# Graph attention layer 1 by four column groups while its gather is still running, the node's own part on ScalarE, and the carry between partitions applied to one fetched row per partition

## The chip, the cores and the metric

The program runs on one core of one Trainium2 chip. The metric is the device time of one execution in microseconds. The kernel before was timed in three runs: median 4706.49 us, lowest 4698.56, highest 4711.57. One further execution was recorded by the hardware profiler; all rows below are from it.

## The reference, cut to what matters

A graph of 100,000 nodes and 25,000 edges sorted by destination passes through four layers (gated, two-head attention twice, cosine attention, message passing), each followed by a layer norm. The change is in the first of the two attention layers:

```python
logits = jax.nn.leaky_relu(alpha_s[src] + alpha_d[dst], 0.2)
m = jax.ops.segment_max(logits, dst, num_segments=N)
e = jnp.exp(logits - m[dst])
s = jax.ops.segment_sum(e, dst, num_segments=N)
a = e / s[dst]
out = jax.ops.segment_sum(h[src] * a[:, :, None], dst, num_segments=N)
```

Every node also has an edge to itself (the "own" part). Only nodes that are a destination of some edge need this work; the others are finished in an earlier, dense pass.

## The kernel before

**Layout.** The 25,000 sorted edges lie as 125 partitions x 200 columns (P, J), 200 consecutive edges per partition. A segment (all edges of one destination) is a run along the columns, and may go on into the next partition. Sums over segments are scans along the columns (`tensor_tensor_scan`) followed by a carry between the partitions: the last column is transposed on TensorE, scanned, and transposed back (`carry_dve`, L829 to L839). `cont`, `last` and `more` mark where runs go on and end, `reach_f` which columns a carry reaches.

**Blocks.** The program is a row of blocks; every engine ends its part of a block before the next block starts. In order: constants and start, degrees (L1030), dense node pass (L1093), gate layer (L1225), attention layer 1 (L1379, the block that is changed), attention layer 2 (L1493), cosine layer (L1591), message layer (L1696).

**The block of attention layer 1.** GpSimd (POOL) gathers one row of 69 floats per edge from the table `x1_rows` into `xa` (a view of `edge_rows`): 8 indirect DMAs for the last 4 partitions (the "tail"), then 200 of 121 rows, one per column (L215), all counted by one semaphore. VectorE (DVE) meanwhile runs the first part of a bitonic sort that a later layer needs (L938 to L989), then `attention_dve` (L1307): it spreads the destination's term (L1312 to L871), waits for the whole gather (L1319), makes segment maxima, exponentials and segment sums over all 200 columns and both heads, and inverts the sums. The gathered rows are weighed by the exponentials, the first 80 columns on GpSimd and the other 120 on VectorE (`weigh1`, L1365, L1366). Then 128 scans, one per head and feature, sum them along the columns (L881), with one carry per head.

After that comes a loop over 25 chunks of 8 columns (NC), two to a loop iteration, with two sets of buffers. For each chunk VectorE does ten operations on 125x512 (own part, carry, sum and division for each head) into `e_dup`; TensorE transposes the eight 125x128 tiles (L1427), ScalarE (ACT) copies them from PSUM (L1450), TensorE multiplies them by `heads_w`, with a bias matmul ahead of every bank (L463, L1437), and ScalarE copies the result out in six pieces (L1458, L1459), whence SyncE (SP) stores it into `h_rows` by two DMAs of 462 KB and 54 KB. The product uses one set of three PSUM banks, so the next product waits for these six copies. SyncE also loads the node's own rows `r_x` for every chunk. Layer 2 gathers from `h_rows`, so its block starts when all is stored.

## Time and profile before

| | |
|---|---|
| median of 3 runs | 4706.49 us (4698.56 to 4711.57) |
| the profiled execution, its own time | 4719.72 us |
| its span, first to last instruction | 4717.9 us |
| busy: TensorE, VectorE, ScalarE, GpSimd | 1437.9, 2476.2, 959.6, 2857.0 us |
| mean granted TensorE clock | 0.529 of full |

Times in rows are microseconds from the start of the span. 1.8 us lie outside the span. A row of a timeline gives start, duration, engine, line, operation, what it writes <- reads, count, and in brackets how long the engine was idle before and who released it. A granted clock of 0.50 is TensorE at 1.2 GHz, 1.00 is 2.4 GHz.

### The profile page before, as it was taken

What the parts mean: (1) busy time and instruction counts of PE and PEld (TensorE: products, weight loads), DVE (VectorE), ACT (ScalarE), POOL (GpSimd) and SP (SyncE); (2) the same over time, 40 slices, a digit from 0 to 9 for tenths busy, and PEclk for the clock granted to TensorE, in tenths of its full rate; (3) what the DMA queues carried; (4) which work ended last, traced back from release to release, by engine and by line L of the source; (5) the groups of instructions that cost most, each with busy time, mean ns of one, the idle gap of its engine ahead of it and who ended that gap; (6) DMA issues with size and microseconds to landing.
All of it is one profiled execution on the core that took longest, in us unless ns stands there. A gap on an engine that the chain in (4) does not pass through costs nothing. (4 is left out here: it accounts for less than half of the span.)

```text
span 4717.9 us, 35071 instructions
## 1 busy us (share of the span) xinstructions
PE 1437.9 (30%) x5413; PEld 1244.8 (26%) x5413; DVE 2476.2 (52%) x5048; ACT 959.6 (20%) x2420; POOL 2857.0 (61%) x2507
## 2 busy tenths in 40 slices
PE   2888067772041002753400000000000067154121
PEld 2888057772030001542300000000000045143121
DVE  4565056661587848762078843334864434352453
ACT  1555034441020000210100011221000034123110
POOL 7777777777205760017750057777248877787687
PEclk8555555555555555555555555555555556556555
DMA  3666145542011100224403345554001145344011
GB/s 81 191 188 186 34 116 139 139 135 48 5 44 39 27 16 20 85 72 104 123 7 90 99 115 141 151 147 127 5 10 19 19 122 161 100 111 112 16 17 17
DMA packets 260931, 398.20 MB, mean 84 GB/s; under 512 B 98227, under 2 KB 104370, under 8 KB 260842
## 3 DMA queue, kind: packets, MB, share of 16 engines
q1 hardware_dynamic: 171022, 322.96, 22.6%
q0 software_dynamic: 89856, 74.77, 9.1%
q14 instruction: 47, 0.39, 0.0%
q8 instruction: 6, 0.10, 0.0%
HBM read 185.60 MB, written 212.64 MB: 84 GB/s over the span
## 5 line engine op out<-in xcount | busy, mean ns | idle before, releaser
L806 PE MATMUL banks<-ident,cross_in 125*2 125x125 f32 (+3 forms) x26 | 10.5, 405 | 2015.3 <-DVE cross_in L829 1366.4
L593 PE MATMUL banks<-node_w,x_t 65*125 65x200 f32 x1600 | 551.5, 536 | 0.0
L806 PEld LDWEIGHTS banks<-ident,cross_in 125*2 125x2 f32 (+3 forms) x26 | 3.0, 117 | 2019.9 <-DVE cross_in L829 1369.5
L593 PEld LDWEIGHTS banks<-node_w,x_t 65*125 65x125 f32 x1600 | 515.1, 330 | 3.9
L215 POOL DMA_INDIRECT edge_rows<-x_rows,src_i x400 | 414.7, 1037 | 127.8 <-issue 127.8
L273 POOL DMA_INDIRECT x_rows<-r_x,src_scat_i x200 | 258.3, 1291 | 120.4 <-issue 60.6
L273 POOL DMA_INDIRECT norm_rows<-edge_rows,scat_i x200 | 259.1, 1295 | 74.2 <-issue 74.2
L273 POOL DMA_INDIRECT out_dram<-n_out,scat_i x200 | 250.3, 1251 | 78.9 <-issue 60.7
L215 POOL DMA_INDIRECT edge_rows<-x_rows,dst_place_i x200 | 231.6, 1158 | 64.5 <-issue 64.5
L215 POOL DMA_INDIRECT edge_rows<-in_x_dram,src_i x200 | 221.8, 1109 | 69.1 <-issue 65.4
L636 DVE TENSOR_REDUCE n_var<-n_sq 125x8 f32<-125x512 f32 x125 | 85.6, 686 | 324.0 <-ACT n_sq L650 323.9
L215 POOL DMA_INDIRECT edge_rows<-in_x_dram,dst_i x200 | 214.7, 1074 | 63.7 <-issue 63.7
L215 POOL DMA_INDIRECT edge_rows<-x_rows,norm_s x200 | 213.1, 1066 | 64.5 <-issue 64.5
L215 POOL DMA_INDIRECT edge_rows<-x_rows,key_i x200 | 213.7, 1068 | 61.0 <-issue 61.0
L215 POOL DMA_INDIRECT tops<-norm_rows,src_i x200 | 207.7, 1038 | 63.7 <-issue 63.7
L215 POOL DMA_INDIRECT edge_rows<-h_rows,src_i x200 | 204.9, 1025 | 63.8 <-issue 63.8
L1146 ACT ACTIVATE n_sq<-n_c 125x512 f32<-125x512 f32 x100 | 62.9, 629 | 828.6 <-DVE n_c L1131 828.6
L236 POOL DMA_INDIRECT x_t<-h_rows,src_tail_i x8 | 8.0, 1006 | 337.0 <-POOLq L1379 334.9
L236 POOL DMA_INDIRECT x_t<-x_rows,gray_i x16 | 16.8, 1052 | 301.5 <-DMA gray_i<-sorted_pairs 296.9
L881 DVE TENSOR_TENSOR_SCAN edge_rows<-cont,edge_rows 125x200 f32<-125x200 f32 x384 | 186.2, 570 | 11.1 <-POOL edge_rows L1373 10.9
L455 PE MATMUL banks<-ident,own 125*65 125x125 f32 x400 | 96.5, 422 | 313.3 <-DVE own L529 313.3
L742 DVE TENSOR_REDUCE n_var<-n_sq 125x8 f32<-125x512 f32 x100 | 68.5, 685 | 220.7 <-ACT n_sq L727 220.7
(346 smaller groups left out, 5045.9 us busy)
## 6 DMA issues: line engine op xcount, KB each, us to landing
h_rows<-r_h SPq DMA_DIRECT2D x125, 462.0 KB
x_rows<-r_x SPq DMA_DIRECT2D x125, 241.5 KB
x_rows<-r_x SPq DMA_DIRECT2D x125, 224.0 KB
r_x<-x_rows SPq DMA_DIRECT2D x125, 224.0 KB
x_rows<-n_out SPq DMA_DIRECT2D x125, 224.0 KB
n_in<-in_x_dram SPq DMA_DIRECT2D x100, 224.0 KB
n_c<-x_rows SPq DMA_DIRECT2D x100, 224.0 KB
out_dram<-n_out SPq DMA_DIRECT2D x100, 224.0 KB
```

Source lines behind the costliest of these rows:

```text
L215: g.indirect_dma_start(out=to[0:MAIN, j, :], out_offset=None, in_=table, in_offset=bass.IndirectOffsetOnAxis(ap=idx[0:MAIN, j:j + 1], axis ...
L236: g.indirect_dma_start(out=self.rows[:, j, :], out_offset=None, in_=self.table, in_offset=bass.IndirectOffsetOnAxis(ap=self.idx[:, j:j + 1 ...
L273: g.indirect_dma_start(out=table, out_offset=bass.IndirectOffsetOnAxis(ap=idx[:, j:j + 1], axis=0), in_=frm[:, j, :] if len(frm.shape) == ...
L455: done = pe.transpose(bank[4 + 2 * u + c // 4][0:D + 1, c % 4 * P:c % 4 * P + P], rows[:, c, :], ident[0:P, 0:P])
L593: done = pe.matmul(product[h][:, n // 2, n % 2, :], x_t[u][:, at:at + P], node_w[:, :], start=True, stop=True)
L636: dve.tensor_reduce(n_var[u][:, :], n_sq[u][:, :, :], AX, ALU.add).then_inc(sx3.var, 1)
L742: dve.tensor_reduce(n_var[u][:, :], n_sq[u][:, :, :], AX, ALU.add).then_inc(so.var, 1)
L806: pe.transpose(bank[0][0:cols, 0:rows], frm, ident[0:rows, 0:rows]).then_inc(s_tout, 1)
L881: done = dve.tensor_tensor_scan(rows[:, :, f], cont[:, :], rows[:, :, f], 0.0, ALU.mult, ALU.add)
L1146: nc.scalar.activation(flat(n_sq[u][:, :, :]), flat(n_c[u][:, :, :]) if frm is None else frm(u), ACT.Square, scale=D ** -0.5).then_inc(s.s ...
```

## The change

1. The block works by four **column groups** of 80, 64, 32 and 24 columns (10, 8, 4 and 3 chunks). The gather counts each group on its own semaphore, and VectorE starts a group when its columns are there. The order of the 200 gathers stays.
2. In each group a **running softmax**: peaks are scanned first, every column's sum is rescaled to the new peak by the scan itself (its multiplier is `scales` instead of `cont`), and a group's scans start from the last column of the group before (a per-partition scalar as initial value). So there are 4 x 128 feature scans of 80, 64, 32 and 24 columns instead of 128 of 200. The spreading of maxima and sums back over the segment is gone. All weighing is on VectorE.
3. `merge_own` makes two factors per column and head: `mixes` for the sum and for the own part.
4. In the chunk, **ScalarE makes the own part**: 16 activations of 125x64, each with a per-partition scale read from `mixes`, into `e_dup`. VectorE does two products (ahead) and two additions. The order on TensorE and ScalarE is written out by hand, chunk by chunk.
5. No carry is added to the chunks. `e_dup` of every chunk is also stored (table ED, 512 KB a chunk). At the end the carry between the partitions is worked out (`ends_in`), **one row per partition** (the first segment end in it, the only one that a carry can change) is fetched from ED by an indirect DMA, mended, multiplied by `heads_w` and scattered over its row in `h_rows`.
6. Elsewhere: `own_logits` (the spreading of the destination's term) goes ahead of the sort; comparisons read the integer keys and save three casts in three blocks; the degree block finds the first segment ends (`first_ends`, nine small operations); the cosine layer uses the same four groups instead of five. 

The core of the diff (blank lines left out, `...` for what is left out; `ends_in` computes maxima and masses of the first segment ends, one carry for the peaks and, for each head, three transposes of 65 rows with one scan):

```diff
-GROUPS = (0, 10, 18, 22, 24, 25)
+GROUPS = (0, 10, 18, 22, 25)
...
+        def running_softmax(dve, s, rows, at, n, sums, weigh):
+            a, b = (NC * c for c in groups[n])
+            c = slice(a, b)
+            for h in range(H):
+                done = dve.tensor_tensor(scales[:, 2 + h, c], rows[:, c, at + h], dens[h][:, c], ALU.add)
+            v.link(done)
+            for h in range(H):
+                done = dve.scalar_tensor_tensor(scales[:, 2 + h, c], scales[:, 2 + h, c], 0.2, scales[:, 2 + h, c], ALU.mult, ALU.max)
+            v.link(done)
+            for h in range(H):
+                done = dve.tensor_tensor_scan(peaks[:, h, a + 1:b + 1], pen_f[:, c], scales[:, 2 + h, c], peaks[:, h, a:a + 1], ALU.add, ALU.max)
+            v.link(done)
+            for h in range(H):
+                dve.tensor_tensor(scales[:, 2 + h, c], scales[:, 2 + h, c], peaks[:, h, a + 1:b + 1], ALU.subtract)
+                done = dve.tensor_tensor(scales[:, h, c], peaks[:, h, a:b], peaks[:, h, a + 1:b + 1], ALU.subtract)
+            v.link(done)
+            for h in range(H):
+                done = dve.scalar_tensor_tensor(scales[:, h, c], scales[:, h, c], 0.0, pen_f[:, c], ALU.min, ALU.add)
+            done.then_inc(s.args, 1)
+            dve.wait_ge(s.exps, 2 * n + 1)
+            for h in range(H):
+                done = dve.tensor_tensor_scan(masses[:, h, c], scales[:, h, c], scales[:, 2 + h, c], masses[:, h, a - 1:a] if a else 0.0, ALU.mult, ALU.add)
+            v.link(weigh(dve, c))
+            for h in range(H):
+                for f in range(D):
+                    done = dve.tensor_tensor_scan(sums[h][:, c, f], scales[:, h, c], sums[h][:, c, f], sums[h][:, a - 1, f:f + 1] if a else 0.0, ALU.mult, ALU.add)
+            v.link(done)
+        def merge_own(dve, s, n, share):
...
+            for k in range(2 * H):
+                done = dve.scalar_tensor_tensor(mixes[:, k, w], mixes[:, k, w], share, scales[:, 2 + k % H, c], ALU.mult, ALU.mult)
+            done.then_inc(s.args, 1)
+            dve.wait_ge(s.args, 3 * n + 3)
...
+        def ends_in(dve, s, sums):
...
-                gather_all(g, tail_xa, s1.gathered, src_place_i)
-                g.wait_ge(s1.gathered, ALL)
-                g.wait_ge(s1.exps, 1)
-                weigh1(g, pool, GPSIMD_COLS).then_inc(s_shared, 1)
+                tail_xa.fetch(g)
+                for n, (start, end) in enumerate(groups):
+                    cols = range(start * NC, end * NC)
+                    gather(g, xa, X1, src_place_i, s_got[n], cols[0:TAIL_STEPS[0]])
+                    if n == 0:
+                        tail_xa.put_down(g)
+                    gather(g, xa, X1, src_place_i, s_got[n], cols[TAIL_STEPS[0]:])
+                    if n == 0:
+                        tail_xa.place(g, s_first)
+                for u in range(U):
+                    g.wait_ge(s1.mixed[u], ROWS_DONE * ((ECH + 1 - u) // 2))
+                g.wait_ge(s1.turned, ECH)
+                g.indirect_dma_start(out=first_mixed.rearrange("p h f -> p (h f)"), out_offset=None, in_=ED,
+                                     in_offset=bass.IndirectOffsetOnAxis(ap=first_i[:, :], axis=0)).then_inc(s_first, 16)
+                for u in range(U):
+                    g.wait_ge(s1.stored[u], ROWS_DONE * ((ECH + 1 - u) // 2))
+                g.wait_ge(s1.row, ECH + 1)
+                g.indirect_dma_start(out=H2, out_offset=bass.IndirectOffsetOnAxis(ap=first_scat_i[:, :], axis=0), in_=first_row, in_offset=None,
+                                     bounds_check=last_row(g, ROWS), oob_is_err=False).then_inc(s_first, 16)
...
                 sort_fill_dve(dve)
+                own_logits(dve)
                 sort_start_dve(dve)
                 sort_dve(dve, PARTS[0], held[0], held[1])
...
+                dve.wait_ge(s_first, 16)
+                for n, (start, end) in enumerate(groups):
+                    dve.wait_ge(s_got[n], got_done(n, 1))
+                    running_softmax(dve, s1, xa, D + 1, n, sums, weigh)
+                    merge_own(dve, s1, n, 1.0)
+                    for i in range(start, end):
+                        u, c, w = i % 2, slice(i * NC, i * NC + NC), slice((i - start) * NC, (i - start) * NC + NC)
+                        parts = (n_sq[u], n_in[u])
+                        for h in range(H):
+                            done = dve.tensor_tensor(parts[h][:, :, :], sums[h][:, c, :], wide(mixes[:, h, w]), ALU.mult)
+                        v.link(done)
+                        dve.wait_ge(s1.own, i + 1)
+                        for h in range(H):
+                            done = dve.tensor_tensor(e_dup[u][:, :, h, :], e_dup[u][:, :, h, :], parts[h][:, :, :], ALU.add)
+                        done.then_inc(s1.x, 1)
+                ends_in(dve, s1, sums)
...
-                    sum_rows_dve(dve, sums[h], carry_rows[h])
-
-                def body(i, us):
-                    for u in us:
-                        dve.wait_ge(s1.loaded[u], ROWS_DONE * i + ROWS_DONE)
-                        if not is_first(i):
-                            dve.wait_ge(s1.turned, 2 * i - 1 + u)
-                        for h in range(H):
-                            tmp = (n_sq, n_in)[h][u][:, :, :]
-                            v.link(dve.tensor_tensor(tmp, r_x1[u][:, :, 0:D], wide(chunk(selfs[h], i, u)), ALU.mult))
-                            add_carry(dve, n_out[u][:, :, :], sums[h], carry_rows[h], i, u, n_c[u][:, :, :])
-                            v.link(dve.tensor_tensor(tmp, tmp, n_out[u][:, :, :], ALU.add))
-                            done = dve.tensor_tensor(e_dup[u][:, :, h, :], tmp, wide(chunk(dens[h], i, u)), ALU.mult)
-                        done.then_inc(s1.x, 1)
-                pairs(nc.vector, ECH, body, v)
+                    dve.tensor_scalar(n_sq[0][:, h, :], first_mixed[:, h, :], first_keep[:, h:h + 1], None, ALU.mult)
...
+                for start, end in groups:
+                    for i in range(start, end):
+                        turn_chunk(i)
+                        if i > start:
+                            heads_chunk(i - 1)
+                    heads_chunk(end - 1)
+                ends_pe(pe)
...
+                def own_chunk(i, start):
+                    u = i % 2
+                    act.wait_ge(s1.loaded[u], ROWS_DONE * (i // 2 + 1))
+                    if i >= 2:
+                        act.wait_ge(s1.turned, i - 1)
+                        act.wait_ge(s1.mixed[u], ROWS_DONE * (i // 2))
+                    for c in range(NC):
+                        w = (i - start) * NC + c
+                        for h in range(H):
+                            done = nc.scalar.activation(e_dup[u][:, c, h, :], r_x1[u][:, c, 0:D], ACT.Copy, scale=mixes[:, 2 + h, w:w + 1])
...
+                for n, (start, end) in enumerate(groups):
+                    logits_act(act, s1, n)
+                    if n:
+                        turned_chunk(start - 1)
+                        row_chunk(start - 1)
+                    merged_act(act, s1, n)
+                    act.wait_ge(s1.args, 3 * n + 3)
+                    for i in range(start, end):
+                        own_chunk(i, start)
+                        if i > start:
+                            turned_chunk(i - 1)
+                            row_chunk(i - 1)
+                turned_chunk(ECH - 1)
+                row_chunk(ECH - 1)
+                ends_act(act, s1)
...
+                for i in range(ECH):
+                    u = i % 2
+                    sp.wait_ge(s1.x, i + 1)
+                    rows_dma(sp, edge_rows(ED, i // 2, u, 2 * D), flat(e_dup[u][:, :, :, :].rearrange("p c h f -> p c (h f)")), s1.mixed[u])
+                    if i + U < ECH:
+                        load(i + U)
+                    sp.wait_ge(s1.row, i + 1)
+                    rows_dma(sp, edge_rows(H2[0:EDGES], i // 2, u, W2ROW), flat(r_h2[u][:, :, :]), s1.stored[u])
```

On ScalarE, in the block of layer 1. Before, the loop's first chunks, 2 copies of each transposed pair for two chunks, then the six copies of a product (`own`, `r_h`):

```order
L1450 COPY n_t<-banks 128x500 [waits s_att1_turned]
L1450 COPY n_t<-banks 128x500
L1450 COPY o_t<-banks 128x500 [waits s_att1_turned]
L1450 COPY o_t<-banks 128x500
L1458 COPY own<-banks 125x12 [waits s_att1_h2]
L1459 COPY r_h<-banks 125x396
L1458 COPY own<-banks 125x12
L1459 COPY r_h<-banks 125x396
L1458 COPY own<-banks 125x8
L1459 COPY r_h<-banks 125x264
```

Now, from the third chunk of a group (`mixed`: its earlier `e_dup` is stored; `loaded`: own rows are there):

```order
L1654 ACTIVATE e_dup<-r_x,x_t 125x64 [waits s_att1_mixed0,s_att1_turned,s_att1_loaded0]
L1654 ACTIVATE e_dup<-r_x,x_t 125x64 x15
L1660 COPY o_t<-banks 128x500 [waits s_att1_turned]
L1660 COPY o_t<-banks 128x500
L1670 COPY own<-banks 125x12 [waits s_att1_h2]
L1671 COPY r_h<-banks 125x396
L1670 COPY own<-banks 125x12
L1671 COPY r_h<-banks 125x396
L1670 COPY own<-banks 125x8
L1671 COPY r_h<-banks 125x264
```

The sixteen activations of chunk i stand ahead of the copies of chunk i-1, and behind those of chunk i-2's product. At a group's start 32 activations (two chunks) stand together.

On TensorE, at the same place; `turned_sb`, `row` and `x` are the semaphores of ScalarE's two sets of copies and of VectorE's `e_dup`. Before, inside the loop (two transposes, two products):

```order
L1427 MATMUL banks<-ident,e_dup 128x125 [waits s_att1_turned_sb,s_att1_x]
L1427 MATMUL banks<-ident,e_dup 128x125 x7
L463 MATMUL banks<-h_bias,ones 125x396 [waits s_att1_row,s_att1_turned_sb]
L1437 MATMUL banks<-heads_w,n_t 125x132 x3
L463 MATMUL banks<-h_bias,ones 125x396
L1437 MATMUL banks<-heads_w,n_t 125x132 x3
L463 MATMUL banks<-h_bias,ones 125x264
L1437 MATMUL banks<-heads_w,n_t 125x132 x2
L463 MATMUL banks<-h_bias,ones 125x396 [waits s_att1_row,s_att1_turned_sb]
L1437 MATMUL banks<-heads_w,o_t 125x132 x3
```

Now:

```order
L1612 MATMUL banks<-ident,e_dup 128x125 [waits s_att1_turned_sb,s_att1_x]
L1612 MATMUL banks<-ident,e_dup 128x125 x7
L464 MATMUL banks<-h_bias,ones 125x396 [waits s_att1_row,s_att1_turned_sb]
L1624 MATMUL banks<-heads_w,o_t 125x132 x3
L464 MATMUL banks<-h_bias,ones 125x396
L1624 MATMUL banks<-heads_w,o_t 125x132 x3
L464 MATMUL banks<-h_bias,ones 125x264
L1624 MATMUL banks<-heads_w,o_t 125x132 x2
```

The transposes of chunk i now stand ahead of the product of chunk i-1, one to one; before, two transposes stood ahead of two products.

## Rows read from the trace of the kernel before

**Rows 1.** VectorE's timeline, block of layer 1 (from 1440 us)

```profile
1455.41 0.29 DVE L946 CAST o_t<-att 128x256 f32<-128x256 int32 x1 [11.74 <-DMA att<-edge_places]
...
1655.25 0.33 DVE L1312 COPY dens_selfs<-own 125x200 f32<-125x200 f32 x1
...
1726.14 0.51 DVE L1319 TENSOR_TENSOR head<-edge_rows,dens_selfs 125x200 f32<-125x200 f32 x1 [63.86 <-DMA edge_rows<-x_rows,src_i]
...
1740.94 9.08 DVE L1334 COPY dens_selfs<-head 125x200 f32<-125x200 f32 x2 [1.21 <-ACT dens_selfs L1345]
...
1766.92 8.16 DVE L1365 TENSOR_TENSOR edge_rows<-edge_rows,head 125x7680 f32<-125x7680 f32 x1
...
1783.31 29.92 DVE L881 TENSOR_TENSOR_SCAN edge_rows<-cont,edge_rows 125x200 f32<-125x200 f32 x64
...
1848.96 0.69 DVE L1407 TENSOR_TENSOR n_sq<-r_x,dens_selfs 125x512 f32<-125x512 f32 x1
```

**Rows 2.** GpSimd's timeline, same block: last gather, first weighing

```profile
1723.43 1.02 POOL L215 DMA_INDIRECT edge_rows<-x_rows,src_i  x1 [0.30 <-issue]
1741.07 8.84 POOL L1365 TENSOR_TENSOR edge_rows<-edge_rows,head 125x5120 f32<-125x5120 f32 x1 [16.62 <-ACT dens_selfs L1345]
```

**Rows 3.** TensorE's timeline in the chunk loop

```profile
1863.13 1.93 PE L1427 MATMUL banks<-ident,e_dup 125*128 125x125 f32 x8 [5.09 <-DVE e_dup L1410]
...
1872.45 0.55 PE L463 MATMUL banks<-h_bias,ones 3*125 3x396 bf16 x1 [1.56 <-ACT r_h L1459]
...
1878.12 2.13 PE L1427 MATMUL banks<-ident,e_dup 125*128 125x125 f32 x16
1880.75 0.38 PE L463 MATMUL banks<-h_bias,ones 3*125 3x396 bf16 x1 [0.51 <-ACT n_t L1450]
```

**Rows 4.** ScalarE's timeline in the chunk loop

```profile
1870.92 0.17 ACT L1458 COPY own<-banks 125x12 f32<-125x12 f32 x1 [4.78 <-PE banks L1437]
...
1884.28 0.17 ACT L1458 COPY own<-banks 125x12 f32 x1 [2.62 <-PE banks L1437]
```

**Rows 5.** Stretches: us; busy (count) of PE, PEld, DVE, ACT, POOL; clock; DMA share; GB/s

```profile
1864.00:1868.00 4.00, 4.00 (x15) 2.76 (x14) 3.67 (x6) 1.05 (x2) 0.00 (x0) 0.50 0.26 69
...
1880.00:1884.00 4.00, 3.49 (x22) 2.40 (x20) 0.00 (x0) 1.66 (x4) 0.00 (x0) 1.00 0.69 198
...
2240.00:2260.00 20.00, 12.47 (x44) 8.89 (x44) 0.00 (x0) 3.88 (x7) 15.43 (x16) 0.50 0.42 115
```

**Rows 6.** VectorE's groups by shape, 1438 to 2095 us: busy, mean ns | idle

```profile
L881 DVE TENSOR_TENSOR_SCAN edge_rows<-cont,edge_rows 125x200 f32<-125x200 f32 x128 | 61.5, 559 | 0.1
...
L832 DVE TENSOR_TENSOR_SCAN crossed<-pass_r_t,banks 2x125 f32<-2x125 f32 x2 | 0.8, 402 | 0.1
L871 DVE SCALAR_TENSOR_TENSOR tops<-reach_r,carry_in,tops 125x200 f32<-125x200 f32 x2 | 0.8, 424 | 0.0
...
L1315 DVE SCALAR_TENSOR_TENSOR dens_selfs<-dens_selfs 125x200 f32<-125x200 f32 x2 | 0.7, 368 | 0.1
```

**Rows 7.** ScalarE's activations, gate layer: timeline (two with a pointer operand)

```profile
1288.90 0.49 ACT L1150 ACTIVATE n_sd<-n_var,eps 125x8 f32<-125x8 f32 x2
```

**Rows 8.** ScalarE's groups by shape, gate layer and layer 1

```profile
L1146 ACT ACTIVATE n_sq<-n_c 125x512 f32<-125x512 f32 x3 | 1.9, 629 | 56.9 <-DVE n_c L1131 56.9
L1150 ACT ACTIVATE n_sd<-n_var,eps 125x8 f32<-125x8 f32 x2 | 0.5, 292 | 0.0
L1345 ACT ACTIVATE head<-head 125x200 f32<-125x200 f32 x2 | 0.6, 362 | 296.1 <-DVE dens_selfs L1330 296.1
```

**Rows 9.** Timeline at the end of the block, VectorE's last `e_dup`, GpSimd's next gather

```profile
2078.22 0.69 DVE L1410 TENSOR_TENSOR e_dup<-n_in,dens_selfs 125x512 f32<-125x512 f32 x1
2093.74 1.04 POOL L236 DMA_INDIRECT x_t<-h_rows,src_tail_i  x1 [334.87 <-POOLq L1379]
```

**Rows 10.** Timeline at the end of the degree block

```profile
69.37 0.26 DVE L1028 CAST scat_i<-head 125x200 int32<-125x200 f32 x1
77.64 1.05 POOL L215 DMA_INDIRECT edge_rows<-in_x_dram,src_i  x1 [3.73 <-POOLq L1030]
```

More of the change, by code:

```diff
@@ L920, in build @@
         held = [t[:, :, :].rearrange("p k f -> p (k f)") for t in (att1, att2)]
-        def turns_before(step):
-            return sum(what == "turn" for what, _ in STEPS[:step])
         def sort_sp(sp):
@@ L953, in sort_dve @@
         def sort_dve(dve, part, to_k, to_d):
-            now, turns = 0, turns_before(part[0])
+            now = 0
             for n in range(*part):
@@ new lines, in logits_act, with merged_act, first_at @@
+        def logits_act(act, s, n):
+            a, b = (NC * c for c in groups[n])
+            act.wait_ge(s.args, 3 * n + 1)
+            nc.scalar.activation(scales[:, :, a:b], scales[:, :, a:b], ACT.Exp).then_inc(s.exps, 1)
+        def merged_act(act, s, n):
+            w = NC * (groups[n][1] - groups[n][0])
+            act.wait_ge(s.args, 3 * n + 2)
+            nc.scalar.activation(mixes[:, :, 0:w], mixes[:, :, 0:w], ACT.Exp).then_inc(s.exps, 1)
+        def first_at(dve, plane_of, to):
+            for h in range(H):
+                v.link(dve.tensor_tensor(heads[h][:, :], plane_of(h), first_end[:, :], ALU.mult))
+                done = dve.tensor_reduce(to[:, h:h + 1], heads[h][:, :], AX, ALU.add)
+            v.link(done)
@@ new lines, in ends_act, with ends_pe @@
+        def ends_act(act, s):
+            act.wait_ge(s.args, 3 * len(groups) + 1)
+            nc.scalar.activation(end_exp, end_exp, ACT.Exp)
+            nc.scalar.activation(first_exp, first_exp, ACT.Exp).then_inc(s.exps, 1)
+        def ends_pe(pe):
+            carry_pe(pe, H, "max")
+            for _ in range(H):
+                transpose_pe(pe, cross_in[0:P, 0:D + 1], P, D + 1)
+                transpose_pe(pe, cross_in[0:P, 0:D + 1], P, D + 1)
+                transpose_pe(pe, crossed[0:D + 1, 0:P], D + 1, P)
@@ L1379, in build @@
+        crossings["bank"] = bank[7]
+        first_mixed, first_row = e_dup[1][:, 0, :, :], r_h2[1][:, 0, :]
         with nc.Block() as block:
@@ new lines, in _ @@
+                done.then_inc(s1.x, 1)
+                v.link(dve.tensor_scalar(heads[0][:, :], first_end[:, :], 1.0, -1.0, ALU.subtract, ALU.mult))
+                dve.wait_ge(s1.row, ECH + 1)
+                for k in range(4):
+                    v.link(dve.tensor_tensor(own4[:, :, k], own4[:, :, k], heads[0][:, :], ALU.mult))
+                for k in range(4):
+                    v.link(dve.scalar_tensor_tensor(own4[:, :, k], first_end[:, :], first_row[:, 2 * D + k:2 * D + k + 1], own4[:, :, k], ALU.mult, ALU.add))
@@ new lines, in heads_chunk @@
+                def heads_chunk(i):
+                    u = i % 2
+                    pe.wait_ge(s1.turned_sb, i + 1)
+                    if i:
+                        pe.wait_ge(s1.row, i)
+                    for c in range(NC):
+                        if c % 3 == 0:
+                            cols = min(3, NC - c) * W2ROW
+                            add_bias(pe, bank[4 + c // 3][0:P, 0:cols], h2_bias[:, 0:cols])
+                        done = pe.matmul(h2_slot(c), turned_pair[u][c // 4][:, c % 4 * P:c % 4 * P + P], heads_w[:, :],
+                                         start=False, stop=c % 3 == 2 or c == NC - 1)
+                    done.then_inc(s1.h2, 1)
@@ new lines, in turned_chunk, with row_chunk @@
+                def turned_chunk(i):
+                    act.wait_ge(s1.turned, i + 1)
+                    for b in range(2):
+                        done = nc.scalar.copy(turned_pair[i % 2][b], bank[2 * (i % 2) + b][:, 0:NC // 2 * P])
+                    done.then_inc(s1.turned_sb, 1)
+                def row_chunk(i):
+                    u = i % 2
+                    act.wait_ge(s1.h2, i + 1)
+                    if i >= 2:
+                        act.wait_ge(s1.stored[u], ROWS_DONE * (i // 2))
+                    for b, cols in enumerate((3, 3, 2)):
+                        at = bank[4 + b][0:P, 0:cols * W2ROW]
+                        nc.scalar.copy(own4[:, i * NC + 3 * b:i * NC + 3 * b + cols, :], at.rearrange("p (c w) -> p c w", w=W2ROW)[:, :, 2 * D:W2ROW])
+                        done = nc.scalar.copy(flat(r_h2[u][:, 3 * b:3 * b + cols, :]), at)
+                    done.then_inc(s1.row, 1)
```

246 lines of the change are left out of this document (148 added, 98 removed).

## The prediction

> **What bounds the kernel now.** I read the timelines of the block that is changed first, since the chain of waits over the whole run only names its last part, and asked which engine each stretch waits for. VectorE sorts until 1655.25 us, needs 7 us to spread the destination's term, and then sits idle for 63.86 us until the gather has landed at 1726.1 [rows 1]; the last of the 200 gathers is issued at 1723.4 [rows 2]. From there VectorE alone sets the pace: softmax, weighing and 128 scans until 1848.96 [rows 1], then 25 chunks until 2078.9, which is 9.2 us a chunk. 14.8 us after the last `e_dup` the next block's first gather starts (2093.74) [rows 9]. Everything after that block is unchanged, so what the change is worth is by how much it moves 2093.74. The reader is to see two prizes: the idle 64 us, and a chunk that costs VectorE ten operations. One more lies hidden: two copies took 9.08 us while GpSimd was weighing [rows 1, 2].
>
> **The change, part by part.** I rebuild the block's time from 1655.2 on, when the sort ends.
>
> *What goes ahead of the sort.* `own_logits` takes about 7 us (1655.25 to 1662.28, where the idle time began). It moves into an idle time of 11.74 us, in which VectorE waits for the keys [rows 1]. So the sort ends as before. Were that cover gone, it would cost 7 us.
>
> *Group phases on VectorE.* Group 1's 80 columns are fetched long before 1655: at 1.32 us a gather, 1655 is some 52 gathers ahead of the last [rows 2], so about 148 columns are there; group 2 needs 144, and groups 3 and 4 come later than 1723 anyway. No group waits for the gather.
> - Scans. 200 columns cost 29.92/64 = 0.467 us from start to start [rows 1], 559 ns each as a single duration; 125 columns took 402 ns [rows 6]. The slope is 157/75 = 2.09 ns a column, which leaves 0.05 us fixed. From the second group on, the initial value is a per-partition scalar: such an operand made a three-operand operation 424 instead of 368 ns [rows 6], so +0.056. 128 scans: 27.8 us at 80 columns, 30.7 at 64, 22.1 at 32, 20.0 at 24: together 100.6. Before: 60 and two carries. Bounds: without the scalar's cost 79; 20% more for short instructions 120.
> - Weighing. 7680 elements took 8.16 us [rows 1]: 10.9, 8.7, 4.4, 3.3 for two heads: 27.3. Before, VectorE paid 16.3 and the collision above.
> - Small operations: about 25 a group, at 368 ns for 200 columns [rows 6] and so some 0.24 us for 80 and 0.18 for 24, with two trips to ScalarE of half a microsecond and two reciprocals: an estimate of 8.4, 7.4, 5.3 and 4.8 us.
>
> That is 46.9, 46.7, 31.7 and 28.0 us.
>
> *A wait that the order on ScalarE adds.* Its exponentials for the next group stand behind the product copies of the last chunk but one. These come 9.1 us after VectorE's last `e_dup` (next paragraph), and VectorE needs only 2.3, 1.6, 1.5 us to get there. So it idles 6.8, 7.5 and 7.6 us at the three later groups.
>
> *The chunk.* VectorE's ten operations become four, two of them ahead. But each engine now stands behind the next one round. TensorE transposes chunk i before the product of i-1, so that product waits for `e_dup` of i; ScalarE makes the own part of i+1 only after it has copied the product of i-1. One turn round:
> - ScalarE, 16 activations with a scale from a pointer. Two with a pointer took 0.49 us, 292 ns each, so 0.198 from start to start at 8 elements [rows 7, 8]; 362 ns at 200 and 629 at 512 elements give 0.86 ns an element [rows 8], so 0.246 at 64. I take 0.24: 3.9 us with the last one's end. Lower bound, from the exponential without its pointer cost: 0.17, 2.8 us.
> - VectorE's two additions of 125x512: 0.61 + 0.69 = 1.3.
> - TensorE, eight transposes and the product: from 1863.13 to ScalarE's first copy at 1870.92, 7.8 us at half clock [rows 3, 4].
> - ScalarE's six copies: 1870.92 to TensorE's next start at 1872.45, less one handover: 1.3 [rows 3, 4].
> - Three handovers: 0.1.
>
> Sum: 14.4 us, against 9.2 before. The first two chunks of a group come faster, since their 32 activations stand together: 5.3 us to the first `e_dup`, 3.9 more to the second. So 8 + 6 + 2 + 1 = 17 full rounds are paid.
>
> *SyncE.* A round stores 512 KB of ED and 528 KB of `h_rows` and loads 276 KB, 1.3 MB. At 198 GB/s [rows 5] that is 6.6 us. What was issued in one round is needed a round later; it lies hidden under 14.4, and would decide at a round of about 9.
>
> *The end.* After the last `e_dup` two products are still to come: 7.8 + 1.3, the copies of the last pair 1.0, the product 5.9: 16.0. Only then is TensorE free for the carries of `ends_in`: eight crossings and some forty small operations, 11.5 us by the crossings and operations above. Fetching the row of ED from 10 us on is hidden by that. The mended row through TensorE and ScalarE: 3. The scatter, one gather's 1.0 us [rows 2] and its landing, beside eight operations on `own4`: 4. Closing the block: 3. Together 37.7, where it was 14.8. Bounds: 30 and 46.
>
> **The sum.** 1655.2; first group 46.9 + 5.3 + 3.9 + 8 x 14.4 = 171.3; second 6.8 + 46.7 + 9.2 + 86.4 = 149.1; third 7.5 + 31.7 + 9.2 + 28.8 = 77.2; fourth 7.6 + 28.0 + 9.2 + 14.4 = 59.2. The last `e_dup` ends at 2112.0, the next block's gather starts at 2149.7 instead of 2093.7: 56 us later. Elsewhere: `first_ends` adds about 2 us to VectorE in the degree block, which ends at 69.6 there, while GpSimd's gathers go on until 73.9 and hold the block [rows 10]; with that cover gone it would cost 2. The three saved casts and one group less in the cosine layer give under 1 us each. The profiled execution took 4719.7, so 4775.7; it lay 13 us above the median, and I forecast against the median: 4706.5 + 56 = **4762**.
>
> **A rule that speaks against it.** In the chunk loop TensorE was busy for 7.8 us on end after 5.09 idle [rows 3], and was granted 0.50 in it [rows 5]; only after the next product, with 1.56 us between, did it get full speed (1.00). In the projections, at 62% busy in short bursts, it stayed at 0.50 [rows 5]. A round has 7.8 busy and 6.6 idle, so I count at half clock. The Trainium skill ("TensorE: Matmul & The Clock Gate", Part 1) says that half rate is the default and sustained work releases it; by that, some rounds would be at 2.4 GHz, which is the first rival.
>
> **Rivals.**
> - *TensorE at full clock in the rounds.* For it: the grants above. Eight transposes then take 1.07 (half of 2.13) and the product 3.53 (1880.75 to 1884.28) [rows 3, 4], 3.2 us less a round; 17 rounds 54, the three idle times 10, the end 6: 70 in all, which is 14 us more than the 56 that the change costs: 4692, on the edge of faster. It decides when four fifths of the rounds are fast (56 of 70). Against it: the burst after 5.09 us of idleness was slow from end to end.
> - *Cheap operands.* If neither the scalar of the scans nor the pointer of the activations costs anything: 21 + 1.1 x 25 = 49 us less, 4713. The rows with such operands speak against it.
> - *The round is longer than its parts*, because ED's stores delay the loads or the activations run at their full 0.33: 2 us more a round, 4800.
> - *The change doesn't do what it says.* The gather is then still waited for. It can't be: 148 columns are there at 1655.
>
> **Chances.** Forecast 0.66, full clock 0.14, cheap operands 0.08, longer round 0.12. 0.3% of this time is 14 us, about what a measurement can tell from no change. Slower by more: forecast and longer round, 0.78. Cheap operands come out at 4713, the same; the full clock lies on the edge and is split, with a little for both together: 0.12 same, 0.10 faster. The range of the likeliest alone, from the bounds of scans, activations and the end, is 4725 to 4800; to 8 in 10 it reaches to the edge of the full clock and of the longer round: 4695 to 4812.
>
> **What would show it.** Right: VectorE starts on the logits of group 1 at about 1655 with no idle time for the gather; full rounds of 14.4 us with VectorE idle for over 10 of them and released by ScalarE; clock 0.50 there; about 7 us idle before the exponentials of groups 2 to 4; the next block at about 2150. Wrong: clocks near 1.00 in the rounds, activations 0.17 apart, scans of 24 columns well off 0.16, or VectorE waiting for `mixed` or `loaded`.

## The result, and the profile after

The changed kernel takes 4757.69 us (median of 3 runs, 4755.54 to 4764.99) against 4706.49: ratio 1.0114, 95% interval 1.0086 to 1.0143, so slower by 51 us. Forecast were 4762 and slower. A repeat gave 1.0097 (1.0069 to 1.0125). On three other chips the kernel before and all versions took 6280 to 6490 us; on the one of them where the changed kernel was timed, the change cost 146 us (below).

The next block's first gather is issued at 2152.18 us, 58.4 later than before [rows 9]; 56.0 were forecast. The two profiled spans differ by 38.0 only, because the profiled execution of before held one gather issue for 19.32 us, late in the program. Timeline of before, GpSimd:

```profile
4146.12 1.18 POOL L215 DMA_INDIRECT edge_rows<-x_rows,dst_place_i  x1 [0.30 <-issue]
4147.30 0.61 POOL L241 DMA_DIRECT2D tail_md<-x_t  x1
4148.21 19.32 POOL L215 DMA_INDIRECT edge_rows<-x_rows,dst_place_i  x1 [0.30 <-issue]
```

That gather was issued 18.3 us later than the usual step would have it, and 38.0 + 18.3 = 56.3. So behind the block of layer 1 the changed kernel gains 2 us on net (58.4 to 56.3), and ahead of it 1.7 (the sort's end, below). The medians differ by 51 and not by 56; the three timed runs of before lie 13 us apart, so these 5 us can't be told from scatter.

The start of the groups, timeline of the changed kernel. VectorE goes from the sort's last copy into the logits with no idle time, where before it waited 63.86 us [rows 1]:

```profile
1653.35 0.29 DVE L987 COPY att<-o_t 128x256 f32<-128x256 f32 x1
1653.55 0.49 DVE L1420 TENSOR_TENSOR x_t<-edge_rows,dens_selfs 125x80 f32<-125x80 f32 x2
...
1832.16 0.59 DVE L1437 TENSOR_TENSOR_SCAN x_t<-x_t 125x64 f32<-125x64 f32 x2 [7.14 <-ACT x_t L1475]
...
1980.91 0.46 DVE L1437 TENSOR_TENSOR_SCAN x_t<-x_t 125x32 f32<-125x32 f32 x2 [7.55 <-ACT x_t L1475]
...
2060.23 0.43 DVE L1437 TENSOR_TENSOR_SCAN x_t<-x_t 125x24 f32<-125x24 f32 x2 [7.65 <-ACT x_t L1475]
```

The three bracketed times are the idle that ScalarE's order adds (forecast 6.8, 7.5, 7.6). VectorE's groups in the block, by shape (busy, mean ns | idle):

```profile
L1441 DVE TENSOR_TENSOR_SCAN edge_rows<-x_t,edge_rows 125x64 f32<-125x64 f32 x128 | 31.4, 340 | 0.0
L1441 DVE TENSOR_TENSOR_SCAN edge_rows<-x_t,edge_rows 125x80 f32<-125x80 f32 x128 | 28.4, 312 | 0.0
L1441 DVE TENSOR_TENSOR_SCAN edge_rows<-x_t,edge_rows 125x32 f32<-125x32 f32 x128 | 23.7, 274 | 0.0
L1441 DVE TENSOR_TENSOR_SCAN edge_rows<-x_t,edge_rows 125x24 f32<-125x24 f32 x128 | 21.9, 272 | 0.0
L1583 DVE TENSOR_TENSOR e_dup<-e_dup,n_sq 125x512 f32<-125x512 f32 x25 | 17.3, 693 | 214.0 <-ACT e_dup L1654 214.0
```

The last row is where the time went: VectorE stood 214 us idle in front of its additions, released each time by ScalarE's own part. One full round, timeline of all engines:

```profile
1736.58 0.69 DVE L1583 TENSOR_TENSOR e_dup<-e_dup,n_sq 125x512 f32<-125x512 f32 x1 [11.92 <-ACT e_dup L1654]
...
1737.93 1.93 PE L1612 MATMUL banks<-ident,e_dup 125*128 125x125 f32 x8 [6.66 <-DVE e_dup L1583]
...
1745.73 0.17 ACT L1670 COPY own<-banks 125x12 f32<-125x12 f32 x1 [8.32 <-PE banks L1624]
...
1746.95 3.95 ACT L1654 ACTIVATE e_dup<-r_x,x_t 125x64 f32<-125x64 f32 x16
...
1751.01 0.69 DVE L1583 TENSOR_TENSOR e_dup<-e_dup,n_sq 125x512 f32<-125x512 f32 x1 [11.92 <-ACT e_dup L1654]
```

Follow the starts: additions, TensorE 1.35 us later, ScalarE's row copies 7.80 after that, the 16 activations 1.22 later, the next additions 4.06 later: 14.43. Each bracket names the one before it, and the activations have none, since ScalarE goes into them straight from its row copies: it is a ring. TensorE's clock in the round before it (stretch; busy of PE, PEld, DVE, ACT, POOL; clock; DMA share; GB/s):

```profile
1723.00:1738.00 15.00, 7.83 (x28) 5.81 (x29) 3.08 (x6) 6.10 (x24) 11.64 (x12) 0.50 0.45 119
```

The end of the block, timeline of the changed kernel:

```profile
2111.84 0.68 DVE L1583 TENSOR_TENSOR e_dup<-e_dup,n_in 125x512 f32<-125x512 f32 x1
...
2127.44 1.21 POOL L1549 DMA_INDIRECT e_dup<-x_mixed_edge_rows,first_i  x1 [368.36 <-DMA x_mixed_edge_rows<-e_dup]
2128.47 0.41 PE L808 MATMUL banks<-ident,cross_in 125*2 125x125 f32 x1
2128.95 0.06 DVE L837 MEMSET crossed<- 2x1 f32 x1 [13.40 <-PE banks L808]
...
2143.61 1.23 POOL L1554 DMA_INDIRECT h_rows<-r_h,first_scat_i  x1 [14.96 <-issue]
2152.18 1.03 POOL L237 DMA_INDIRECT x_t<-h_rows,src_tail_i  x1 [7.34 <-POOLq L1533]
```

The last `e_dup` is done at 2112.5 (forecast 2112.0); the carries stand 13.40 us behind two products; 39.7 us to the next gather (forecast 37.7).

### The profile page after: what moved, and what is told of

Its sections match the earlier page's. It is cut to its first block and busy times, and to the rows that moved or that the text cites. A ratio compares the mean times of both kernels' runs of the same rounds, so it can differ in the third digit from the quotient of the medians.

```text
span 4755.9 us, 35197 instructions
## 1 busy us (share of the span) xinstructions
PE 1450.2 (30%) x5415; PEld 1250.0 (26%) x5415; DVE 2424.0 (51%) x5411; ACT 1056.3 (22%) x2828; POOL 2858.5 (60%) x2507
## 5 line engine op out<-in xcount | busy, mean ns | idle before, releaser
L808 PE MATMUL banks<-ident,cross_in 125*2 125x125 f32 (+4 forms) x26 | 10.9, 419 | 1829.1 <-DVE cross_in L831 1180.1
L216 POOL DMA_INDIRECT edge_rows<-x_rows,src_i x400 | 453.6, 1134 | 125.3 <-issue 125.3
L216 POOL DMA_INDIRECT edge_rows<-x_rows,dst_place_i x200 | 214.5, 1073 | 63.9 <-issue 63.9
L1163 PE MATMUL banks<-ident,n_in 125*128 125x125 f32 x200 | 54.1, 428 | 386.5 <-DVE n_in L1968 282.5
```

What stands on the lines that cost most here:

```text
L216: g.indirect_dma_start(out=to[0:MAIN, j, :], out_offset=None, in_=table, in_offset=bass.IndirectOffsetOnAxis(ap=idx[0:MAIN, j:j + 1], axis ...
L808: pe.transpose(crossings["bank"][0:cols, 0:rows], frm, ident[0:rows, 0:rows]).then_inc(s_tout, 1)
L1163: done = pe.transpose(to[:, c * P:(c + 1) * P], flat(frm[:, 2 * c:2 * c + 2, :]), ident[0:P, 0:P])
```

## The experiments

"Block" is from the first transposes of layer 1 to the next block's first gather: 445.2 us in the changed kernel, 441.8 in its repeat. A round is given from one chunk's transposes to the next one's. Eight of the twelve runs fell on chips where the kernel before took 6304 to 6346 us; there rounds and blocks are compared rather than totals. The block can be compared between the chips: the changed kernel's is 444.7 us on such a chip. A thirteenth kernel, without the stores of the mixed rows (`e_dup`), gave no result.

**Own part ahead (`e1_own_ahead`).** ScalarE's order:

```diff
-    for i in range(start, end):
+    for i in range(start, min(start + 2, end)):
         own_chunk(i, start)
-        if i > start:
-            turned_chunk(i - 1)
-            row_chunk(i - 1)
+    for i in range(start, end - 1):
+        turned_chunk(i)
+        if i + 2 < end:
+            own_chunk(i + 2, start)
+        row_chunk(i)
```

> ScalarE writes the own part of chunk i+2 before it copies out the rows of chunk i, so two chunks' own parts are ready at the start of a group; nothing is left out. Theory A (the round of 14.42 us is a ring of order: own part 3.9, two additions 1.3, transposes and product 7.8, row copies 1.3, each waiting for the one before): the own part leaves the ring, and what is left of it is product 5.9, row copies 1.3, transposed copies 1.05, about 8.4 us. But SyncE still issues the store of the mixed rows of chunk i behind the rows of chunk i-1, and the own part of i+2 waits for that store (issued 2.3 us after the row copies, landing near 5): round 10.3 to 10.8, so 17 rounds give 4757.7 - 17*3.9 = about 4692 (4685 to 4700). Rival B (the stores of the mixed rows do not bind, only ScalarE's order does): about 4657, the same as the next kernel. Rival C (the group phases and the tail are the cost, the rounds are covered): 4755 to 4760.

Measured: rounds of 11.6 to 12.2 us behind a first one of 13.4 to 14.0, block 392.6, 49 less than the repeat's. The time on this chip was 6380.17 against 6306.56, ratio 1.0108 (1.0066 to 1.0149). The ring is broken, but a second one binds: 10.3 to 10.8 us and 66 us less were expected, with the wait for the mixed store as its last link. That link was wrong. Timeline:

```profile
2476.48 3.93 ACT L1654 ACTIVATE e_dup<-r_x,x_t 125x64 f32<-125x64 f32 x16 [5.84 <-DMA r_x<-x_rows]
```

ScalarE waits for the load of the own rows (`r_x`), the last of the three transfers that SyncE issues after the row copies, not for the mixed store ahead of it; it does so for 5.4 to 6.1 us in every full round but the first.

**Store and load first (`e1b_own_ahead_store_first`).** As above, and on SyncE:

```diff
...
         load(i + U)
-    sp.wait_ge(s1.row, i + 1)
-    rows_dma(sp, edge_rows(H2[0:EDGES], i // 2, u, W2ROW), flat(r_h2[u][:, :, :]), s1.stored[u])
+    if i:
+        store(i - 1)
+store(ECH - 1)
```

> As the kernel before, and SyncE issues the mixed store and the next load of chunk i before the row store of chunk i-1; nothing is left out. Theory A: round 8.4 to 8.6 us, 17 * 5.9 = 100 us less: 4657 (4645 to 4670), which is below the kernel before the change (4706.5). Rival D (1.3 MB of loads and stores in a round are what binds then): a round of 10 or more, over 4680. Rival E (TensorE, now busy 7.8 of 8.5 us, is granted its full clock): a round of about 6.5, under 4635. Rival C: 4755 to 4760.

(`store(i)` is the two lines that are taken out.) Measured: rounds of 6.7 to 8.3, block 335.0: 107 less, where 100 were expected. Stretch of its first group:

```profile
2433.00:2507.00 74.00, 63.94 (x251) 48.72 (x251) 25.27 (x49) 52.73 (x207) 0.00 (x0) 0.68 0.53 164
```

TensorE is busy 86% and is now the bound; a part of its work got the full clock (mean 0.68), so that single rounds came down to 6.7; 8.4 to 8.6 were expected. DMA moves 164 GB/s instead of 119. ScalarE still waits for a load of own rows once in each group, 1.35 to 2.21 us at its third chunk, 7.2 us in all, and TensorE doesn't stand still for it. So the mixed store doesn't bind here; whether a kernel without it would be faster isn't shown. The same kernel was run once more on another chip (`e1c_store_first_again`); its block was 332.6.

> The store-first kernel unaltered, to have its time beside a kernel before of about 4707 us. From the traces: first transposes to the next block's first gather 335 us in it and 441.8 us in the repeat of the changed kernel, so 107 us less than that one's 4753.6: 4647 (4638 to 4656), ratio 0.987. Rival D (what the rounds give is lost in the rest of the program): over 4680.

On that chip the kernel before took 6304.48: 6317.53, ratio 1.0018 (0.9997 to 1.0038), and 6313.35 with 1.0005 (0.9981 to 1.0029) the first time. So the expected total of 4647 stays untested.

**Own part on VectorE (`e2_own_on_vector`).**

```diff
+    dve.wait_ge(s1.loaded[u], ROWS_DONE * (i // 2 + 1))
...
+    for h in range(H):
+        done = dve.tensor_tensor(e_dup[u][:, :, h, :], r_x1[u][:, :, 0:D], wide(mixes[:, 2 + h, w]), ALU.mult)
     v.link(done)
-    dve.wait_ge(s1.own, i + 1)
...
-        own_chunk(i, start)
```

> The own part is written by two products of 125x512 on VectorE (0.69 us each) in place of the 16 activations on ScalarE; orders of TensorE, ScalarE and SyncE stay, nothing is left out. Theory A: ScalarE's part leaves the ring and VectorE runs ahead of it; round 8.4 to 9.3, group starts 2 us shorter each: 4757.7 - 17*5.5 - 8 = about 4656 (4640 to 4675). Rival F (the ring is the one-to-one order of TensorE and the row copies, whoever writes the own part): 4757.7 - 17*1.3 = 4735 or more, for 3.9 us on ScalarE become 2.6 on VectorE in the same ring.

Measured: mostly rounds of 10.7 and 7.6 in turn, mean 8.9 over the 17; block 350.9, 91 less; ratio 1.0044 beside 1.0089 and 1.0108 of the two that keep a ring through ScalarE. The own part costs VectorE 1.29 us here and the round is 5.5 us shorter, so what it cost before was its place in ScalarE's order. What is left is VectorE's wait for the same late load (6.8 to 8.6 us in the longer rounds).

**Two activations (`e3_two_activations`).**

```diff
-    for c in range(NC):
-        w = (i - start) * NC + c
-        for h in range(H):
-            done = nc.scalar.activation(e_dup[u][:, c, h, :], r_x1[u][:, c, 0:D], ACT.Copy, scale=mixes[:, 2 + h, w:w + 1])
+    w = (i - start) * NC
+    for h in range(H):
+        done = nc.scalar.activation(e_dup[u][:, :, h, :], r_x1[u][:, :, 0:D], ACT.Copy, scale=mixes[:, 2 + h, w:w + 1])
```

> The own part of a chunk is written by 2 activations of 125x512 (0.63 us each) instead of 16 of 125x64, all 8 columns of a chunk scaled by the first column's weight, so the own part of seven of eight columns is wrongly weighted; order unchanged. Theory A: the ring loses 3.95 - 1.26 = 2.7 us: round 11.7, 17 rounds 46 us, group starts 3.9 us each, 16: 4696 (4688 to 4705). Rival C (ScalarE's time is not in the ring): 4755 to 4760. Rival G (the ring is set by waits for the store of mixed rows, not by ScalarE's work): above 4735.

This kernel leaves out the factors of seven of eight columns, so its results are wrong; the amount of data is the same. Measured: rounds of 11.86 (forecast 11.7) while the clock was 0.50, 10.1 to 10.2 in the second half of group 2, where it was 0.61 on the mean; block 385.3, 56 less. The two activations take 1.40 us instead of 3.95: 2.55 less, and the round is 2.56 shorter. The own part is in the ring with its full length.

**The changed kernel again (`c0_changed_again`, `c1_changed_third`).**

> The changed kernel itself, unaltered, as the mark for the other runs (the first four ran on a chip on which the kernel before took 6306.56 us, not 4706.49). On the chip of the first measurement the ratio was 1.0114, 51 us. If the 51 us come from the layer-1 block alone, as the prediction has it, the absolute difference is about 55 us on any chip (ratio 1.009 at 6306 us, 1.0115 at 4706 us); if the code of the changed kernel, with its loops written out, costs more where instructions arrive late, the difference grows: from the four runs, with 109 us between this kernel's block and that of the store-first kernel, it would be 6313 + 109 = 6422, ratio 1.018.

4753.61 against 4707.20, 46 us, block 441.8.

> The changed kernel itself once more. On a chip where the kernel before takes about 6305 us: the store-first kernel had 6313.35 and 6317.53 there and its block is 107 us shorter than this one's, so 6422 (6405 to 6440), ratio 1.019, a difference of 118 us where the other chip shows 46 to 51: the code written out in 25 chunks and 512 scans then costs some 65 us more where instructions come late. Rival: the difference stays what the block's own steps give, 45 to 60 us, ratio 1.007 to 1.010. On a chip where the kernel before takes about 4707 us: 4755, ratio 1.0097 to 1.0114 as measured twice.

6491.79 against 6345.80: ratio 1.0229 (1.0204 to 1.0255), 146 us where 118 were expected. Its block is 444.7, as on the quicker chips, so the code written out in the chunks isn't what costs more; that part of the expectation was wrong. What differs lies ahead of it. Timeline of that run:

```profile
2309.22 1.01 POOL L216 DMA_INDIRECT edge_rows<-x_rows,src_i  x1 [0.30 <-issue]
```

is its last gather, and VectorE's first logits start at 2433.82. There the sort ends 124 us after the gather, on the first chip 105 us before it (1653.5 against 1758.1). While GpSimd gathers (2046 to 2310 us), VectorE is busy for 77 of 264 us, and afterwards for 98 of 124. The kernel before has the same sort and gather, so the wait of 64 us that the change removes probably wasn't there. 51 + 64 = 115, of the 146; no trace of the kernel before was taken on such a chip, so this is argued, not shown, and 31 us stay open. On the other two such chips the store-first kernel was 7 and 13 us slower than before with a block 110 and 112 us shorter than this one, which gives an estimate of 117 and 125 us for the change.

**Early exponentials (`e5_early_exps`).**

```diff
-    logits_act(act, s1, n)
+    if n == 0:
+        logits_act(act, s1, n)
...
         turned_chunk(i - 1)
+        if i == end - 1 and n + 1 < len(groups):
+            logits_act(act, s1, n + 1)
         row_chunk(i - 1)
```

> Only the place of the three exps of groups 2 to 4 on ScalarE moves: ahead of the row copies of the chunk before the group's last, instead of behind them; nothing is left out. Theory (the idle of 7.14, 7.55 and 7.65 us on VectorE before the scans of groups 2 to 4 is this order and nothing else): those become 0.5 each, and the time falls by 20 to 21 us (18 to 24) against the changed kernel; the rounds of 14.42 stay. Rival H (the ring of the last chunks must finish anyway, and the group after it waits for ScalarE later): the idle moves to the exps of the merge or to the first own part, and the time falls by less than 8.

```profile
1827.89 0.59 DVE L1437 TENSOR_TENSOR_SCAN x_t<-x_t 125x64 f32<-125x64 f32 x2 [0.48 <-ACT x_t L1475]
```

7.14 us became 0.48, and 0.38 and 0.35 are left in groups 3 and 4. Block 423.7, 18 less than the repeat's (21 less than the first run's); 4738.90, which is 15 less, below the 18 to 24 expected. Most of the idle time came back as time, so it hadn't moved elsewhere; the time itself scattered by 22 us over seven runs.

**Three groups (`e6_three_groups`).** `groups = [(0, 10), (10, 18), (18, 25)]` for layer 1.

> Layer 1 runs in three groups of 10, 8 and 7 chunks instead of 10, 8, 4 and 3 (the cosine layer keeps its four); nothing is left out. Theory: one group phase less, from 2050.7 to the first e_dup at 2094.2 (43.5 us), against two full rounds of 14.4 in place of a start, (14.4 + 14.4 - 3.9 = 24.9) and some 6 us more in the scans of the last group: 12 to 13 us less than the changed kernel (8 to 16). If a group's phase were hidden behind other work: 25 us more, not less.

4743.41, 10 us less, in the expected range of 8 to 16; block 437.1, only 5 less than the repeat's and 8 less than the first run's. A group phase isn't hidden, which would have cost 25 us more; its price is shown no closer than that.

**All orders (`e8_all_orders`).** Own part ahead, store and load first, early exponentials and three groups together, and on TensorE the crossings of the carries (`steps`) one by one between the parts of the last two products:

```diff
+                        if i == ECH - 1:
+                            steps = ends_steps(pe)
+                            steps.pop(0)()
+                            heads_chunk(i - 1, steps)
+                            steps.pop(0)()
...
-                ends_pe(pe)
+                heads_chunk(ECH - 1, steps)
+                for step in steps:
+                    step()
```

> Everything together: own part two chunks ahead, mixed store and load ahead of the row store, early exps, three groups, and the carries' transposes put between the three parts of the last two chunks' products instead of behind them; nothing is left out. From the store-first kernel's trace: block 109 us shorter than that of the changed kernel; early exps 15 (two transitions), three groups 19 + 7 (its idle), carries between the products 7: 157 us less than the changed kernel (140 to 170), which is 100 us less than the kernel before, ratio about 0.978 at 4706 us. Rival: the gains share one cover (TensorE at 7.8 us a round is the bound) and the last three give less than half: 120 to 135 less than the changed kernel.

Measured 4606.76 (4593.46 to 4609.94) against 4707.20: ratio **0.9783** (0.9756 to 0.9810), 147 us less than the changed kernel and 100 less than before; block 287.1. 140 to 170 less were expected. The end took 32.9 us from the last transposes instead of 39.6; about 1 us of that is TensorE's clock, since the same order took 34.1 at the half clock (`e10`, below). Nothing of the computation is left out, and this version is faster than both.

**Filler on TensorE (`e11_filler_in_rounds`, `e10_filler_in_groups`).**

```diff
+                def fill(times):
+                    for _ in range(times):
+                        pe.transpose(bank[7][0:P, 0:P], ident[0:P, 0:P], ident[0:P, 0:P])
```

> The changed kernel with 26 transposes of the identity into an unused bank in each of the 17 full rounds on TensorE, behind the product of chunk i-1 and ahead of the transposes of chunk i+1, where TensorE now waits 6.65 us; they are 6.3 us of work at the lower clock; nothing is left out and their result isn't read. Theory K (the granted clock follows TensorE's own activity, and the rounds ran at 0.50 since it was idle almost half of each): the clock goes to 1.00 in the rounds, and a round becomes 14.4 - 3.9 = 10.5: 17 * 3.9 = 66 us less than the changed kernel, 4688 (4680 to 4700), the price of the rival in the prediction on TensorE's clock. Rival: the clock stays at 0.50 or rises for a part of the rounds only; the rounds stay at 14.4 to 14.8 and the time at 4750 to 4765.

Stretch of the first group:

```profile
2436.00:2546.00 110.00, 82.56 (x432) 69.01 (x431) 22.14 (x36) 51.83 (x204) 0.00 (x0) 0.80 0.33 102
```

The clock rose to 0.80 on the mean, not to 1.00: most rounds took 12.6 to 13.5, some 14.4, and two, in which transposes and product ran wholly at the full clock, 10.96 and 10.97 (10.5 expected). The mean may be high: the profile gives 1.00 from 2439 to 2454 us too, where the eight transposes took 1.93. In the next round after each the transposes were back at 1.93 us, the half clock. Block 422.4, 19 less instead of 66; 6417.35 against 6304.48, ratio 1.0158 (1.0127 to 1.0189). So the clock rival is a real mechanism, worth 3.5 us a round (3.2 in the prediction), but only in the rounds that get it.

> The kernel with all orders moved, and 200 transposes of the identity into an unused bank on TensorE ahead of each of the three groups' first transposes, 48 us of work at the lower clock and 24 at the full one, while VectorE is in the group's phase; nothing is left out. In the traces TensorE is the bound of its rounds (7.8 us at 0.50; means 0.61, 0.67 and 0.71 over the three groups). Theory K: the rounds start at the full clock, and then the bound is ScalarE with 1.3 + 1.05 + 3.95 = 6.3 us: up to 22 * 1.2 = 26 us less, about 4583 (4575 to 4595) against 4606.8. Rival: the clock is back at 0.50 by the first transposes, or falls again in the rounds, and the time stays at 4600 to 4612; where the filler outlasts VectorE's phase, the groups start later and it is over 4612.

No gain. Block 299.3 against 287.1 without filler; 6282.62 against 6304.48, ratio 0.9959 (0.9934 to 0.9983), on a chip on which the version without filler was not timed. First group, behind the filler and in the chunks:

```profile
2400.00:2436.00 36.00, 0.00 (x0) 0.00 (x0) 32.52 (x144) 4.71 (x19) 0.00 (x0) 0.50 0.00 0
2437.00:2505.00 68.00, 59.10 (x231) 45.42 (x232) 24.04 (x45) 50.63 (x201) 0.00 (x0) 0.58 0.52 159
```

The filler itself ran at the full clock (112 transposes in 12.39 us), so it was 24 us of work and not 48. TensorE had run out of it 45, 15 and 11 us before the three groups' first transposes, and the clock stood at 0.50 when the chunks began. A longer filler wasn't tried, so what a clock kept high would give these rounds stays open.

## Why the prediction held

- *No group waits for the gather, and `own_logits` is hidden:* right. The wait for the keys fell from 11.74 [rows 1] to 5.04 us and the sort ended at 1653.5 (1655.2 forecast).
- *Group phases:* the prediction's parts add up to 47.1, 46.8, 31.8 and 28.1 us, 0.5 more than it states. Measured were 48.0, 47.5, 33.9 and 30.5 us without the waits. The scans are 105.4 us where 100.6 were expected; the term for short ones was 9% too small (21.9 for 24 columns, 20.0 expected). That a scalar as initial value costs time shows in the rows: 64 columns with one took 31.4/128 = 0.245 us, 80 columns without 0.222.
- *The order on ScalarE:* 22.3 us in three idle times, 21.9 forecast. Shown by `e5`.
- *The round:* 14.42 us against 14.4, with the parts on or near their numbers (7.80 for 7.8, 1.22 for 1.3, 1.35 for 1.3, 4.06 with the handover for 3.9). That it is a ring and not a sum of costs, and that the own part's place is the cause, is shown by `e1b`, `e2` and `e3` together: shortening the own part by 2.55 us shortens the round by 2.56; taking it out of the ring takes 5 to 7.
- *The end:* 39.7 against 37.7. The 13.40 us behind the products are the largest part; crossings between them got 5 to 7 of the 40 back (`e10`, `e8`). The prediction's own terms add up to 37.5.
- *Transfers:* that they would decide at a round of about 9 us was wrong: `e1b` has rounds of 7.8 at 164 GB/s. It changed nothing at 14.4.
- That the block's end came out within 3 us is partly luck: the phases were 6.6 us longer than forecast and the end 2.0, the sort ended 1.7 earlier, and four of the 17 full rounds took 12.6 to 13.7 us, 5 us less in all. In the repeat, one stretch of full rounds had a granted clock of 0.50, and a short one, of 12.66 us, 0.63:

```profile
1763.00:1792.00 29.00, 15.70 (x55) 11.66 (x56) 5.17 (x9) 12.18 (x48) 0.00 (x0) 0.50 0.30 92
1791.00:1804.50 13.50, 6.03 (x28) 4.62 (x28) 3.34 (x7) 6.39 (x25) 0.00 (x0) 0.63 0.37 119
```

- *Rivals.* The full clock came in a part of four rounds (granted 0.62 to 0.77 in them) and was worth 5 us, not 70. The Trainium skill ("TensorE: Matmul & The Clock Gate", Part 1) says that activity releases the half rate; the trace agrees for these four, while in thirteen rounds with the same 7.8 us of work on end it stayed at 0.50. Cheap operands and a longer round are both out: the pointer activations cost what the rows said, and no wait on `mixed` or `loaded`, which ScalarE and not VectorE would have, shows in the rounds.
- Not foreseen: the prediction weighed the gain of 64 us as fixed. It is the distance between the ends of two independent chains, and should go where the sort is slower; no trace of the kernel before shows that.

## What to carry to other kernels

Before splitting a chunk's work over three engines, write down for each engine which chunk its next instruction belongs to, and go round: if the chain returns to its start one chunk on, the round is the sum of all stages, however idle each engine is. The remedy is one place in an order (here two chunks ahead on ScalarE, and the transfers that it needs ahead of those that it doesn't on SyncE), and was worth 107 us of the block where the whole change had cost 51 of the time. A wait taken away is worth what it is on the chip and in the run at hand; look at what ends the two chains that met there.

## What the runs showed of the hardware

**A long run on VectorE can hold a gather's issue on GpSimd.** Timeline of GpSimd in the changed kernel, while VectorE weighs (two operations of 5.47 and 5.49 us) and then runs 128 scans from 1668.39 to 1696.8:

```profile
1658.36 5.36 POOL L216 DMA_INDIRECT edge_rows<-x_rows,src_i  x1 [0.31 <-issue]
1664.03 5.22 POOL L216 DMA_INDIRECT edge_rows<-x_rows,src_i  x1 [0.30 <-issue]
1669.55 1.12 POOL L216 DMA_INDIRECT edge_rows<-x_rows,src_i  x1 [0.30 <-issue]
1670.98 1.64 POOL L216 DMA_INDIRECT edge_rows<-x_rows,src_i  x1 [0.30 <-issue]
1672.92 24.78 POOL L216 DMA_INDIRECT edge_rows<-x_rows,src_i  x1 [0.30 <-issue]
1698.01 1.02 POOL L216 DMA_INDIRECT edge_rows<-x_rows,src_i  x1 [0.31 <-issue]
```

The long one ends 0.9 us after the last scan. Not every issue is held: the third and the fourth took 1.12 and 1.64 us beside the same scans. All five traces of such kernels on the faster chips have it (24.58, 28.13, 26.53 and 28.17 us in the others), and so do 19.32 us of the kernel before and 16.45 in `e6_three_groups`, both in the message block beside scans of 200 columns, and both ending 0.9 us after the last of them. The Trainium skill ("SBUF — State Buffer", Who interferes with whom) says that VectorE's 2-port modes keep GpSimd from writing descriptors, and infers that a `tensor_tensor`, which has two inputs and no such mode, doesn't; the two issues beside the weighing (5.36 and 5.22 us instead of 1.02) say that it can. The same section of the Trainium skill has an operation with two SBUF inputs contend with GpSimd's reads. These gathers read their index list from SBUF, so that may be the way; no run here tests it. Here it cost the gather 32 us and the kernel nothing, since group 2 begins 63 us after the last gather. A kernel that waits for its gather would pay for it.

**Chips on which instructions come late.** On three chips the kernel before, the changed one and its variants took 6280 to 6490 us. Durations are nearly the same (below, 556.3 us of work against 551.8 in the repeat); engines stand idle with nothing to wait for, most of it in stretches in which GpSimd issues gathers: in the stretch from 70 to 600 us TensorE is busy for 76 us in `c1_changed_third` and for 349 in the repeat. TensorE's projections in `c1_changed_third`, which had 0.0 idle in the repeat:

```profile
L594 PE MATMUL banks<-node_w,x_t 65*125 65x200 f32 x1600 | 556.3, 537 | 661.6 <-issue 658.3 <-ACT r_h L569 3.3
```

What holds the instructions up, these runs don't show.
